# A graph network of four layers: early splits and first gathers, and a new order in the edge steps

## The reference, cut to what matters

```python
x = _layernorm(x + _L0(x, edge_index, ...))                 # two GAT convolutions (512 -> 1024 -> 1024), then @ Wfc + bfc
x = _layernorm(x + relu(segment_sum((x @ weight)[src] * edge_weight[:, None], dst)))      # L1
x = _layernorm(x + _L2(x, src, dst, edge_attr_20, edge_weight, edge_attr_4, ...))         # PaiNN-like messages
x = _layernorm(x + segment_sum(relu(concat(x[src], x[dst]) @ W.T + b), src))              # L3
```

## Time and profile before

| | |
|---|---|
| median of 3 runs | 2535.97 us (2528.84 to 2541.94) |
| the profiled execution | 2555.53 us, its span 2553.5 us, mean granted TensorE clock 0.952 |
| TensorE busy | 2341.6 us (92%) |
| VectorE busy | 1527.5 us (60%) |
| ScalarE busy | 996.9 us (39%) |
| GpSimd busy | 1020.3 us (40%) |
| DMA | 394.21 MB, 154 GB/s over the span |
| first stage, second stage | 0 to 553 us, 553 us to the end |

### The profile page before, as it was taken

The page is one execution under the profiler, slowest core; times in us unless marked ns, Lnnn a source line. Parts: engine busy times, 40 slices in busy tenths (PEclk is TensorE's granted clock), DMA queues, the critical chain, the costliest instruction groups (busy, mean ns, idle before and its releaser), DMA issues.

```text
span 2553.5 us, 33436 instructions
## 1 busy us (share of the span) xinstructions
PE 2341.6 (92%) x10787; PEld 1879.7 (74%) x10787; DVE 1527.5 (60%) x4649; ACT 996.9 (39%) x2005; POOL 1020.3 (40%) x971
## 2 busy tenths in 40 slices
PE   6977699968999999899989999999998988989997
PEld 5855488856888888777768888888876766767775
DVE  6745377743666854333326664588776775767654
ACT  5942012211256632121214664334335544545343
POOL 2042606627032234345532222157664545542532
PEclk8987799988999999999989999999999989999998
DMA  5423155552267732222225665566665646554432
GB/s 181 142 98 105 47 187 184 178 158 62 77 216 250 255 125 92 73 70 92 77 65 178 238 232 181 165 212 215 205 207 186 210 165 196 191 175 159 151 109 68
DMA packets 171539, 394.21 MB, mean 154 GB/s; under 512 B 44967, under 2 KB 73902, under 8 KB 170830
## 3 DMA queue, kind: packets, MB, share of 16 engines
q0 software_dynamic: 65296, 184.67, 23.1%
q1 hardware_dynamic: 106090, 207.66, 23.1%
HBM read 221.98 MB, written 170.25 MB: 154 GB/s over the span
## 4 chain that ended last, share of the span: by engine, by line
PE 63%; DVE 6%; issue 5%; ACT 2%; DMA 1%; POOL 0%; another core or an unknown queue 0%; DVEq 0%; ACTq 0%; POOLq 0%
PE g_h_ps L2443 12%; PE g_h_ps L2445 12%; PE g_h_ps L2444 12%; PE g_t_ps L2424 5%; PE g_h_ps L2468 4%; PE g_h_ps L2470 4%; PE g_h_ps L2469 4%; PE g_h_ps L1715 1%; PE g_h_ps L1713 1%; PE g_h_ps L1714 1%; DVE g_x_hi L2693 1%; PE g_sum_ps L965 1%; PE g_sum_ps L966 1%; PE g_misc_ps L1457 1%; PE g_h_ps L1725 1%
## 5 line engine op out<-in xcount | busy, mean ns | idle before, releaser
L2443 PE MATMUL g_h_ps<-held_w_hi,g_x_hi 128*128 128x512 f32 x1264 | 519.3, 411 | 14.6 <-issue 11.8
L2445 PE MATMUL g_h_ps<-held_w_hi,g_x_lo 128*128 128x512 f32 x1264 | 502.1, 397 | 13.5 <-issue 13.3
L2444 PE MATMUL g_h_ps<-held_w_lo,g_x_hi 128*128 128x512 f32 x1264 | 501.0, 396 | 13.3 <-issue 13.0
L2545 ACT ACTIVATE g_act_t<-g_t_ps,g_b_col 128x256 f32<-128x256 f32 (+1 forms) x640 | 264.2, 467 | 482.8 <-PE g_t_ps L2424 352.4
L2693 DVE CAST g_x_hi<-g_act_t 128x512 fp32r<-128x512 f32 (+1 forms) x320 | 151.1, 472 | 299.3 <-ACT g_act_t L2545 240.5
L594 DVE CUSTOM_DVE_ANT_0 g_prod<-g_h_sb,g_a_rows 128x256 f32<-128x256 f32 x632 | 224.7, 422 | 169.4 <-ACT g_h_sb L492 143.9
L2445 PEld LDWEIGHTS g_h_ps<-held_w_hi,g_x_lo 128*128 128x128 f32 x1264 | 241.5, 191 | 71.2 <-issue 18.4
L2443 PEld LDWEIGHTS g_h_ps<-held_w_hi,g_x_hi 128*128 128x128 f32 x1264 | 241.7, 191 | 63.9 <-issue 17.3
L423 PE MATMUL g_h_ps<-g_w_hi,g_x_hi 128*128 128x512 f32 x616 | 247.7, 402 | 44.5 <-issue 19.2
L2444 PEld LDWEIGHTS g_h_ps<-held_w_lo,g_x_hi 128*128 128x128 f32 x1264 | 242.2, 192 | 61.8 <-issue 18.3
L2468 PE MATMUL g_h_ps<-fc_w_hi,g_x_hi 128*128 128x512 f32 x632 | 280.7, 444 | 1.2 <-DVE g_x_lo L2695 0.7
(11 more groups left out here) (386 smaller groups left out, 4134.9 us busy)
## 6 DMA issues: line engine op xcount, KB each, us to landing
h<-g_h_sb SPq DMA_DIRECT2D x158, 512.0 KB
g_x_in<-h SPq DMA_DIRECT2D x59, 512.0 KB
g_x_in<-in_dram SPq DMA_DIRECT2D x40, 512.0 KB
h<-g_rows_own SPq DMA_DIRECT2D x40, 512.0 KB
x<-fc_x SPq DMA_DIRECT2D x20, 512.0 KB
x<-conv_x SPq DMA_DIRECT2D x20, 512.0 KB
g_w_raw<-in_dram SPq DMA_DIRECT2D x12, 512.0 KB, 4.8
fc_w_raw<-in_dram SPq DMA_DIRECT2D x20, 256.0 KB
```

Source lines behind the costliest of these rows:

```text
L2443: pe.matmul(out, xh, wh, start=(k == 0), stop=False)
L2444: pe.matmul(out, xh, wl, start=False, stop=False)
L2445: last = pe.matmul(out, xl, wh, start=False, stop=(k == KC - 1))
L2545: last = act.activation(act_t[:, k, 0:width], t_ps[f % 2][:, c, 0:width], ACT.Relu, bias=b_col[:, m // GM, k:k + 1])
```

## The change

It changes the order of work in five places; nothing is computed otherwise.

- First stage, VectorE: `splits` of macro tiles 1 and 2 stand each ahead of one row conversion, and `body(0)` does no splits.
- Second stage, start: Pool issues the first four gathers before it makes its constants; SyncE sends the broadcast of `a_rows` only when these gathers have landed, and `b_rows` at h = WFC (150), ahead of the first FC weight load; the first products wait for each pair of chunks instead of for all.
- Convolution steps, VectorE: z's addition is a function of its own, `add`, and `split_sums` comes between it and `factors`.
- PaiNN steps, TensorE: `turn_x` and `out_one` move to part 1, in this order, ahead of `sum_edges`; ScalarE: `copy_xt` and `copy_hidden` move to part 1 ahead of `copy_sums`, `softplus` behind it.
- PaiNN steps, VectorE: `scalars` moves from part 1 to part 2, behind the messages.

```diff
@@ first stage, VectorE, body(i) and ahead of it
-                    splits(2 * i + 1, i, 1)
+                    if not first(i):
+                        splits(2 * i + 1, i, 1)
                     attention(2 * i, i, 0)
-                    if not last:
+                    if not (last or first(i)):
                         splits(2 * i + 2, i + 1, 0)
                     attention(2 * i + 1, i, 1)
...
                 for o in range(2):
+                    splits(o + 1, (o + 1) // 2, (o + 1) % 2)
                     dve.wait_ge(rows_in[o], 16)
@@ class ConvEdges
+    def add(self, dve, t):
+        h, q = self.hold, t % 2
+        dve.wait_ge(self.multiplied, t + 1)
+        if t >= 2:
+            dve.wait_ge(self.y_done, t - 1)
+        dve.scalar_tensor_tensor(h.z[q][:, :], h.y_ps[q], 0.0, h.x_dst[t % self.ROWS], ALU.max, ALU.add).then_inc(self.z_done, 1)
+
     def factors(self, dve, t):
         h, q, n0 = self.hold, t % 2, self.LN_STEPS * t
-        (the same wait and addition)
@@ second stage, SyncE
+                for s in range(2):
+                    for j in range(2):
+                        sp.wait_ge(x_loaded[s][j], 16)
                 sp.dma_start(a_rows[:, :, :], avec.partition_broadcast(P)).then_inc(a_in, 16)
-                for j in range(2):
-                    sp.dma_start(b_rows[:, j, :], b_out.partition_broadcast(P)).then_inc(b_rows_in, 16)
...
+                    if h == WFC:
+                        for j in range(2):
+                            sp.dma_start(b_rows[:, j, :], b_out.partition_broadcast(P)).then_inc(b_rows_in, 16)
                     if WFC <= h < WFC + KC:
                         load_fc(h - WFC)
@@ Pool: the block of memset, affine_select and iota (L2244 to L2250) moves behind
                 gather(0)
                 gather(1)
@@ TensorE, products(h)
-                    if h == first_half[m]:
+                    if h and h == first_half[m]:
                         pe.wait_ge(lo_done, FILLS * (m + 1))
...
                     for k in range(KC):
+                        if h == 0:
+                            pe.wait_ge(lo_done, k // 2 + 1)
@@ TensorE, beside(g)
                         if 0 <= n - 2 < ET:
                             painn.out_two(pe, n - 2)
+                    if part == 1:
+                        if 0 <= n + 2 < ET:
+                            painn.turn_x(pe, n + 2)
                         if 0 <= n < ET:
                             painn.out_one(pe, n)
-                        if 0 <= n + 2 < ET:
-                            painn.turn_x(pe, n + 2)
-                    if part == 1 and 0 <= n + 1 < ET:
-                        painn.sum_edges(pe, n + 1)
+                        if 0 <= n + 1 < ET:
+                            painn.sum_edges(pe, n + 1)
@@ ScalarE, beside(g)
                             painn.copy_sums_t(act, n)
-                            painn.copy_hidden(act, n)
-                        if 0 <= n < ET and n % 2 == 1:
-                            painn.softplus(act, n // 2)
-                        if 0 <= n + 2 < ET:
-                            painn.copy_xt(act, n + 2)
...
                     if part == 1:
+                        if 0 <= n + 2 < ET:
+                            painn.copy_xt(act, n + 2)
+                        if 0 <= n < ET:
+                            painn.copy_hidden(act, n)
                         if 0 <= n + 1 < ET:
                             painn.copy_sums(act, n + 1)
+                        if 0 <= n < ET and n % 2 == 1:
+                            painn.softplus(act, n // 2)
@@ VectorE, beside(g)
                         if 0 <= n < ET:
-                            conv.factors(dve, n)
+                            conv.add(dve, n)
                         if 0 <= n + 1 < ET:
                             conv.split_sums(dve, n + 1)
                         if 0 <= n < ET:
+                            conv.factors(dve, n)
                             conv.shifts(dve, n)
...
-                    if part == 1 and n % 2 == 1 and 0 <= n < ET:
-                        painn.scalars(dve, n // 2)
...
                             painn.messages(dve, n + 2)
+                        if n % 2 == 1 and 0 <= n < ET:
+                            painn.scalars(dve, n // 2)
```

18 lines of the change are left out of this document (9 added, 9 removed).

## The result

| | median us | runs |
|---|---|---|
| kernel before | 2528.4 (2516.4 to 2541.9) | 20 |
| changed kernel | 2541.4 (2526.8 to 2547.8) | 20 |
| ratio | 1.0041, 95% interval 1.0025 to 1.0056 | |

The forecast was 2519 with a range of 2503 to 2538; the changed kernel is slower by 0.41%, 10 us (13 by the medians). That is a small loss, but its interval doesn't reach zero, and the forecast was a gain of 17 us. The two profiled executions say the opposite: 2555.5 us before, 2540.1 after. The first is the odd one. So the two traces can be compared step by step, but their spans can't.

The account below looks back on a forecast made before the run. TensorE bounds the kernel (63% of the chain), so only shorter TensorE stalls pay. The terms -0.3 - 6.1 - 8.2 - 2.4 sum to -17.0 us: 2538.5 profiled, 2519.0 for the median, range 2503 to 2538.

Parts of the forecast that it names:

- C: Convolution steps: splitting the sums right behind z's addition shortens TensorE's waits for `conv_t_lo`, -8.2 us, bounds -13 to -2.
- B: Second stage's start: earlier gathers, broadcasts held back, first product waiting pair by pair; -6.1 us, bounds 2 to 9 gained.
- "given back" rival: Gathers need their 10 us anyway, convolution gaps become waits for ScalarE's late ReLU, PaiNN gains zero: -7 us, 2529; chance 0.35.
- Part A: First stage: early splits move TensorE's 13.1 us wait to tile 1's second half; net 0.3 us less.
- takes its 7.25 us as before: First stage: the second row's load is issued 1.9 us later by the inserted split, but its duration stays 7.25 us.
- Landing and order: Second stage's start: first gather issued 1.1 us earlier, and 2.5 us from broadcasts leaving the gathers' window; 3.6 us gained.
- the wait pair by pair: Second stage: the first product waits for one split pair instead of four, 2.5 us gained, all on the path.
- it will begin at 1947.71, 1.98 us earlier: Convolution step at 1947: the split, at 1949.69 before, follows z's addition directly; 1.4 us taken off each long wait.
- the prediction's list of signs: What the profile would show if right or wrong, such as `conv_t_lo` waits near 6 us or over 10 us for `painn_scal`.
- The lost cover: Convolution steps: ScalarE's root instructions no longer run beside the split, leaving VectorE about 0.6 us idle a step.
- Part D: PaiNN steps: odd-step waits lose 5.7 us, new even-step stalls cost 1.3 and grown old waits 2.0; -2.4 us.
- softplus rival: PaiNN steps: `out_two` waiting for `scalars` becomes the bound, 3.5 us a step; +12.2 us in all, 2548; chance 0.06.

Follow-up runs that it names:

- A+C+D: The changed kernel without the changes to the second stage's start, against the kernel before: ratio 0.9991, 2402.7 us where the kernel before takes 2405.1.
- B alone: The kernel before with only the second stage's start changed: ratio 1.0031 to the kernel before, which takes 2528.9 us on that chip.
- A+B+D: The changed kernel without the convolution's part, against the kernel before: 0.9918 where that takes 2405.1 us, 1.0012 where it takes 2530.2.

## Why the prediction was wrong

Two steps of the sum failed: C's -8.2, which is +4 to +8, and B's -6.1, which on chips with stalls beside Pool's rows is not kept.

**The sum's missing term.** One failed step is a term that isn't there: the sum took the time that lay beside Pool's rows for granted. The earlier trace rows were chosen from a list that also had 96.7 us of "issue" waits. What brings TensorE earlier into such a stretch can lose it there. The "given back" rival looked for B's loss in the gathers' latency, not beside Pool's rows.

**Part A** (-0.3, bounds -2.2 to +1.5): the mechanism holds to the number. The wait of 13.09 moved to the second half of tile 1 as 11.70 at 40.28, and the last piece of the counting began at 148.12 instead of 147.47. The second row was converted at 31.47 instead of 28.46: 1.6 us from the inserted split, the rest because the load took 8.67 us, not 7.25. The term "takes its 7.25 us as before" is the mis-sized one: over all traces the load took 7.12 to 8.92 us with A (median 8.0) and 6.95 to 7.34 without. The rule that the prediction cites, that a VectorE copy holds back Pool's descriptors, is borne out for the issue itself. It takes 0.54 us in 16 traces. In the other four, where VectorE's cast of x begins 0.04 to 0.21 us into it, it takes 0.85 to 1.02 us and ends 0.12 us behind the cast each time, as here in A+C+D (in a fifth the cast begins 0.25 us into it, and it takes 0.54):

```profile
22.83 1.02 POOL L340 DMA_DIRECT2D g_early_signs<-in_dram  x1 [13.39 <-DVE g_early_row L645]
23.04 0.69 DVE L578 CAST g_x_hi<-g_x_in 128x1024 fp32r<-128x1024 f32 x1 [0.51 <-PE g_h_ps L407]
```

So the price is up to 0.5 us, and whether it falls due hangs on some tenths. The earlier trace rows are a weaker case than the prediction made them: the issue between its two, at 471.82, took 1.55 us beside VectorE's subtraction and no copy. What the prediction didn't follow is the wait at 234 us, the first place where TensorE's lead meets a VectorE chain that depends on Pool, and the fall of the clock behind it.

**Part B** (-6.1, bounds 2 to 9): its terms are right and rather small. Landing and order gave 4.8 us (11.6 to 6.8 from Pool's first instruction of the stage to the transposes; 3.6 predicted), the wait pair by pair 2.8 (2.5 predicted). Where no stall follows it is kept: -8.0 in the trace and -10.2 by medians on the 2405 us chip, -7.7 to -9.5 in the three pairs of traces with pauses. On the 2528.9 us chip B alone is *slower*, by 8 us (1 to 14). Shown is that the stalls beside the row decide what B is worth in a trace, since pauses bring its gain back. Not shown is why B alone is a loss: a stalled trace loses some 5 to 11 us more than the others, which takes B's 8 to 10 us away but doesn't turn them into +8, and only half of the traces are stalled. That stays open.

**Part C** (-8.2, bounds -13 to -2): wrong in sign, +4 to +8. The failed step is "it will begin at 1947.71, 1.98 us earlier" with the 1.4 us off each long wait that follow from it. It treated the split as the end of the chain. It isn't: the waits for `conv_t_lo` are 15.8 us in all, not the 6 of the prediction's list of signs; on the 2530.2 us chip the three long ones are 5.3, 3.7 and 2.6 us in A+B+D and 5.1, 3.4 and 2.3 in the changed kernel. What the split gains within a step, the next step's later start takes, as the pair of steps above shows. The lost cover was named, at 0.6 us a step, and it is there (0.51). What the sum left out is the larger part: statistics and factors now stand behind the split, so root, normalizing, ReLU and the next tile's splits are all 2.7 us later measured from it. The "given back" rival had the right place, a late ReLU, and its sign, transposes that wait for `g_act_t` in these steps, came true; it still priced C at -3.

**Part D** (-2.4, bounds -13 to the softplus rival): right direction, size off where nothing disturbs it. On the 2405 us chip the 15.1 us of `out_one` became 11.1 of `out_two`, and the trace gains 7.6 us from 1900 on. On the 2528.9 us chip it gives -2 us, with an interval across zero. The softplus rival's place was right: `out_two` waits for `scalars` 9.8 us in ten steps of the changed kernel, at most 3.3, just under the 10 that the prediction set as a sign of being wrong, and three times the 1.3 + 2.0 of the sum. Its 3.5 us in every step was not. The direction holds because all twelve old waits went, 14.5 us, where the sum took out 5.7.

**The base.** The sum was made against an execution that was itself 27 us over its kernel's later median. Taking 19.5 off left the gains as they were. Those were read elsewhere in the trace than in its odd stretch, and the same waits stand in the other traces, so this moved the forecast's level and not its difference.

## What to carry to other kernels

When a waits list has a large "issue" entry, look at it before anything else. First see whether another engine's instruction ends just ahead of each: then it is a plain wait that the view didn't name. If not, and it stands beside a long row of small DMAs of Pool, try breaking the row up; here a pause cost 1.4 to 6.8 us, and all pauses together gave 3%. Don't move work ahead on one engine without following what it is now ahead *of* to the next engine's in-order queue; a split that comes sooner and a normalizing that comes later are one edit. And take two or three profiles of the kernel before: a plan read from a single execution prices things that the others don't have.

## What the hardware showed that was not expected

- A row of 40 scatters without a pause slows TensorE from some 28 us after its start until it ends (151.9, 179.8 and 205.5 to 208 us in one trace of A+B+D), on four chips of five. Pauses of 1.4 to 5.7 us after every tenth take TensorE's busy time between 150 and 320 us from 125 to 159 of 170 us, and the granted clock from 0.82 to 0.98 with it.
- Chips differ in this. On four, the kernel before takes 2529 to 2533 us, on one 2405, where the same rows cause no "issue" wait at all. With pauses in all rows two of the four come down to 2440 and 2453. Why the fifth needs none stays open; no paused kernel ran on it.
- Pool stops too: at the second stage's start, in all seven traces of the stalling chips without pauses and without long stalls, its row has a gap of 2.7 to 3.3 us and an issue of 3.9 to 4.3 instead of 0.95; in the three with long stalls it has no such issue and no gap over 1.7 us. What stops it was not tried.
- An issue of Pool in whose first 0.21 us VectorE's cast began ended 0.12 us behind the cast, up to 0.5 us late (four traces); one whose cast began at 0.25 us was not delayed.
